# Vision tower, attention stage: the second layer norm's scaled rows computed by ScalarE instead of VectorE, and the output projection of a group issued one group later on TensorE

## The reference

```python
h = tok(x)                                   # (16, 37, 256)
h = h + attn(layernorm(h), w_qkv, w_o)       # 16 heads of 16, rotary, causal, softmax, @ w_o
h = h + ffn(layernorm(h), ...)               # gated MLP + product-key experts (top 8 of 4096)

def layernorm(x, eps=1e-5):
    return (x - mean(x)) / sqrt(var(x) + eps)
```

## Time and profile before

| | us |
|---|---|
| median of 3 plain runs | 273.3 (273.24 to 273.79) |
| profiled execution | 275.31 |
| its span, first to last instruction | 273.5 |
| busy PE / PEld / DVE / ACT / POOL | 247.0 / 203.7 / 180.7 / 57.0 / 54.7 |
| chain that ended last, shares | PE 58%, DVE 34%, ACT 3%, issue 3%, DMA 1% |
| mean granted TensorE clock | 0.975 of full |

### The profile page before, as it was taken

One profiled execution on the slowest core, in us unless ns is written; L12 is line 12 of the kernel. 1 busy time (PEld: TensorE's weight loads), 2 busy tenths in 40 slices (PEclk: granted clock), 3 DMA queues, 4 the chain that ended last, 5 costly groups with the idle time before them and its releaser, 6 DMA issues.

```text
span 273.5 us, 4832 instructions
## 1 busy us (share of the span) xinstructions
PE 247.0 (90%) x1956; PEld 203.7 (74%) x1956; DVE 180.7 (66%) x455; ACT 57.0 (21%) x104; POOL 54.7 (20%) x71
## 2 busy tenths in 40 slices
PE   3998985889768899899999999899979999999996
PEld 2575653668543488889898899888968888888773
DVE  0037199678885449999999999799968767511100
ACT  1101127343444242323132743100000000000000
POOL 5013146114422523225052620000000000000000
PEclk9999999999975799999999999999999999999999
DMA  7960000130002271061125430300000000000000
GB/s 253 386 233 0 2 0 0 55 104 29 25 20 74 63 218 54 7 205 60 40 54 178 127 105 1 91 0 2 0 19 2 0 19 2 0 19 2 19 0 12
DMA packets 14805, 16.99 MB, mean 62 GB/s; under 512 B 848, under 2 KB 12992, under 8 KB 14784
## 3 DMA queue, kind: packets, MB, share of 16 engines
q1 hardware_dynamic: 13776, 15.70, 17.9%
q10 hardware_dynamic: 1008, 1.00, 1.1%
HBM read 15.48 MB, written 1.21 MB: 61 GB/s over the span
## 4 chain that ended last, share of the span: by engine, by line
PE 58%; DVE 34%; issue 3%; ACT 3%; DMA 1%; DVEq 0%; POOL 0%; ACTq 0%
PE ps L1067 23%; PE ps L1030 9%; PE ps L820 7%; PE ps L1089 5%; DVE topi L696 3%; DVE big L795 3%; DVE top L693 3%; PE ps L971 3%; PE ps L1064 3%; DVE big L547 2%; PE ps L897 2%; DVE xn L515 2%; PE ps L938 2%; PE ps L847 2%; DVE red L589 1%
## 5 line engine op out<-in xcount | busy, mean ns | idle before, releaser
L1067 PE MATMUL ps<-ue,big 128*128 128x256 f32 (+1 forms) x320 | 72.3, 381 | 1.4 <-DVE big L795 1.4
L1067 PEld LDWEIGHTS ps<-ue,big 128*128 128x128 f32 (+1 forms) x320 | 57.2, 182 | 12.1 <-DVE big L795 1.8
L1030 PE MATMUL ps<-hn_hi,de_hi 128*128 128x296 f32 x128 | 40.7, 318 | 2.1 <-ACT big L482 1.1
L795 DVE TENSOR_TENSOR big<-ps,big 128x1024 f32<-128x1024 f32 (+1 forms) x19 | 22.7, 1197 | 26.9 <-PE ps L1089 26.2
L1030 PE MATMUL ps<-hn_lo,de_hi 128*128 128x296 f32 x128 | 38.4, 300 | 0.0
L1030 PE MATMUL ps<-hn_hi,de_lo 128*128 128x296 f32 x128 | 38.2, 299 | 0.0
L482 ACT ACTIVATE big<-ps 128x592 f32<-128x592 f32 x32 | 21.1, 665 | 44.5 <-PE ps L1030 44.4
L1030 PEld LDWEIGHTS ps<-hn_hi,de_hi 128*128 128x128 f32 x128 | 24.1, 188 | 4.7 <-DVE actT L742 1.9
L1030 PEld LDWEIGHTS ps<-hn_lo,de_hi 128*128 128x128 f32 x128 | 24.1, 188 | 1.2 <-issue 1.2
L1030 PEld LDWEIGHTS ps<-hn_hi,de_lo 128*128 128x128 f32 x128 | 24.1, 188 | 0.0
L820 PE MATMUL ps<-big 128*111 128x256 f32 (+1 forms) x72 | 19.3, 426 | 4.7 <-DMA big<-in_w_tok 4.7
(11 more groups left out here) (113 smaller groups left out, 337.9 us busy)
## 6 DMA issues: line engine op xcount, KB each, us to landing
de<-in_down_t SPq DMA_DIRECT2D x16, 256.0 KB, 2.8
ue<-in_up_e SPq DMA_DIRECT2D x4, 1024.0 KB, 5.9
big<-in_patches SPq DMA_DIRECT2D x6, 296.0 KB, 5.2
big<-in_w_tok ACTq DMA_DIRECT2D x6, 128.0 KB, 5.9
big<-in_w_qkv SPq DMA_DIRECT2D x1, 768.0 KB, 8.6
h_scratch<-big SPq DMA_DIRECT2D x5, 111.0 KB
late<-in_keys_bd SPq DMA_DIRECT2D x1, 512.0 KB, 9.7
downT<-in_wdown_t SPq DMA_DIRECT2D x1, 512.0 KB, 9.3
```

The source lines that it names most:

```text
L795: chain(nc.vector.tensor_tensor(dst, pv, dst, ALU.mult), g_ready)
L1030: last = mm(ps[:, 2 + 2 * (e % 2) + a, 0:HALF], half[:, (e // 2) % SPLITS, k, own], src[:, k, a * HALF:(a + 1) * HALF], start=(n == 0), st ...
L1067: last = mm(acc, sil[:, e, j * 128:j * 128 + Q * v], ue[:, e, :], start=False, stop=(e == EX - 1))
```

## The change

VectorE's `hidden_norm` goes. In its place POOL computes, after `rstd`, the value -mean times `rs` into a new tile `shift` (two one-column instructions, `rowshift`), and ACT computes `rs * h + shift` with one activation of the function Identity into `xn`. POOL runs `probabilities` one group further ahead of `rstd`. On PE `project` moves behind the scores of the next iteration, and `hidden_T` comes an iteration later; DVE's `hidden` and ACT's `hn_copy` follow. `hidden(g)` gets a wait for `hn_ready` before it overwrites `mv` and, through POOL, `rs` of two groups earlier.

```diff
 # POOL
+            def rowshift(gi):
+                r = GROUPS[gi][1] * S
+                nc.gpsimd.tensor_scalar(shift[0:r, gi % 2, 0:1], mv[0:r, gi % 2, 0:1], -1.0, None, ALU.mult
+                                        ).then_inc(shift_chain, 1)
+                pool.wait_ge(rstd_ready, NG + gi + 1)
+                pool.wait_ge(shift_chain, gi + 1)
+                nc.gpsimd.tensor_tensor(shift[0:r, gi % 2, 1:2], shift[0:r, gi % 2, 0:1], rs[0:r, gi % 2, :],
+                                        ALU.mult).then_inc(shift_ready, 1)
...
                     probabilities(0)
+                    probabilities(1)
                     for gi in range(NG):
-                        if gi + 1 < NG:
-                            probabilities(gi + 1)
+                        if gi + 2 < NG:
+                            probabilities(gi + 2)
                         rstd(NG + gi, gi)
+                        rowshift(gi)
 # ACT
+            def hidden_norm(gi):
+                r = GROUPS[gi][1] * S
+                act.wait_ge(shift_ready, gi + 1)
+                if gi >= 2:
+                    act.wait_ge(pe_hn, gi - 1)
+                nc.scalar.activation(xn[0:r, gi % 2, :], h[0:r, gi, :], ACT.Identity, bias=shift[0:r, gi % 2, 1:2],
+                                     scale=rs[0:r, gi % 2, :]).then_inc(hn_ready, 1)
...
-                if gi >= 2:
-                    hn_copy(gi - 2)
                 if gi + 2 < NG:
                     exponentials(gi + 2)
-
+                if gi >= 3:
+                    hn_copy(gi - 3)
+                if gi >= 2:
+                    hidden_norm(gi - 2)
+
+            hn_copy(NG - 3)
+            hidden_norm(NG - 2)
             hn_copy(NG - 2)
             act.wait_ge(s_zero, 2)
             for p in range(2):
                 act.wait_ge(pe_q, p + 1)
                 nc.scalar.copy(qT[:, p, 0:BANK], ps[:, 2 + p, :]).then_inc(qT_ready, 1)
+            hidden_norm(NG - 1)
             hn_copy(NG - 1)
 # DVE
                 chain(nc.vector.tensor_tensor(h[0:r, gi, :], ps[0:r, 7, 0:D], h[0:r, gi, :], ALU.add), h_ready)
+                if gi >= 2:
+                    dve.wait_ge(hn_ready, gi - 1)
                 moments(NG + gi, r, h[0:r, gi, :])
...
                 softmax_back(gi)
-                if gi >= 2:
-                    hidden_norm(gi - 2)
                 if gi + 1 < NG:
                     softmax_front(gi + 1)
                 else:
                     gated_rest(0)
                     gated_rest(1)
-                hidden(gi - 1)
-            hidden_norm(NG - 2)
+                if gi >= 2:
+                    hidden(gi - 2)
+            hidden(NG - 2)
             hidden(NG - 1)
             gated_rest(2)
-            hidden_norm(NG - 1)
             gated_rest(3)
 # PE
                 probs_T(gi)
-                if gi >= 2:
-                    hidden_T(gi - 2)
                 if gi + 2 < NG:
                     scores(gi + 2)
+                if gi >= 1:
+                    project(gi - 1)
+                if gi >= 3:
+                    hidden_T(gi - 3)
                 attend(gi)
-                project(gi)
+            hidden_T(NG - 3)
+            project(NG - 1)
             hidden_T(NG - 2)
```

More of the change, by code:

```diff
@@ L185, in vit_tower @@
         rs = sb("rs", [128, 2, 1])
+        shift = sb("shift", [128, 2, 2])
         veps, nhalf = sb("veps", [128, 2, 1]), sb("nhalf", [128, 1])
@@ L233, in vit_tower @@
         var_ready, rstd_ready = sem("var_ready"), sem("rstd_ready")
+        shift_chain, shift_ready = sem("shift_chain"), sem("shift_ready")
         dve_chain, pool_chain = sem("dve_chain"), sem("pool_chain")
@@ L610, in hidden @@
                 chain(nc.vector.tensor_tensor(h[0:r, gi, :], ps[0:r, 7, 0:D], h[0:r, gi, :], ALU.add), h_ready)
+                if gi >= 2:
+                    dve.wait_ge(hn_ready, gi - 1)
                 moments(NG + gi, r, h[0:r, gi, :])
-            def hidden_norm(gi):
-                r = GROUPS[gi][1] * S
-                if gi >= 2:
-                    dve.wait_ge(pe_hn, gi - 1)
-                scaled(NG + gi, r, h[0:r, gi, :], xn[0:r, gi % 2, :], hn_ready)
             def gated_rest(u):
```

## The result

The forecast was 1.8 us faster. The changed kernel is slower: 277.37 us as the median of six plain runs (274.71 to 278.07) against 273.31 (273.24 to 274.91), ratio 1.0114, 95% interval 1.0077 to 1.0151. Its profiled execution took 277.91 with a span of 276.1 (before 273.5).

The account below looks back on a forecast made before the run. VectorE, at 5.49 us a period, was taken to bound the loop. Queries at 84.4 + 6.1 + 1.7 + 1.12 = 93.3 against 95.05 gains 1.8, so 271.5 us from 273.3; range 267.4 to 273.2.

Parts of the forecast that it names:

- the 0.44: TensorE's idle time before project in each loop iteration, waiting for ScalarE's copy; claimed to go, making an iteration 4.61.
- the 1.43: VectorE's loop: time from the start of the second norm's scaling to the next maximum; its removal makes the period 4.06.
- The length of queries: First queries behind the loop, kept at its old 6.1 us; 3.7 at full clock, 7.4 all at the low level.
- The shift pair: GpSimd's two new one-column instructions per group, put at 0.44 to 1.14 us and taken as 0.80.
- The step that failed: Loop's tail: low clock from about 78 adds 0.95 on project(5) and some 0.4 behind it; queries at 84.0 before turns.
- 1.7 + 1.12: Tail: second queries starts 1.7 after the first ends, 0.8 later than before, and takes 1.12.
- the prediction's own sign of being wrong: Behind the second queries: an expert stage that does not move with them would show the forecast wrong.
- Taking turns: VectorE's gate subtractions of 75.0 to 76.9 meeting GpSimd's probabilities(5): 0.85 if they take turns, 0.4 taken.
- Full turns: Rival: gate subtractions and probabilities(5) take turns in full, all behind h_ready(3) 0.45 later than forecast, 271.9; chance 0.13.
- Slower: Rival: clock falls a group sooner, at the wait before transposes(4), 71.5 to 72.3; 1.5 lost, 274.8; chance 0.09.
- nothing comes of it: Rival: project's idle goes, but TensorE waits as long for GpSimd and later hidden rows eat the lead; 273.3; chance 0.06.
- The 0.2%: Some 0.55 us of the whole time, taken as what a measurement can tell from no change; chance within it 0.07.

Follow-up runs that it names:

- casts early: Changed kernel with group 5's scaling ahead of the copies of queries and ScalarE's four gate and up casts in groups 1 and 2; 273.77 us, ratio 0.9985.
- subtractions late: Changed kernel with group 5's scaling ahead of the copies of queries and VectorE's first two gate subtractions behind group 4's residual add; 272.24 us, ratio 0.9928.
- all waits filled: Changed kernel with extra unused matmuls in TensorE's waits over 0.6 us from group 5 on, also between the queries; 270.40 us, ratio 0.9860.
- mended kernel: Changed kernel, group 5's scaling and the casts earlier, two gate subtractions later, project(5) before group 3's hidden transposes; 271.97 us; A: attend(3) start to first queries.
- order alone: Changed kernel's lists, TensorE's new order included, with the scaling back on VectorE; 274.82 us, ratio 1.0019 to the kernel before.

## Why the prediction was wrong

*Right.* VectorE as the bound of the loop, the 0.44 and the 1.43 that go, no table loads, the schedule to attend of group 4 within 0.3, the fall of the clock near 78. The length of queries (6.18, forecast 6.1) was partly luck: it started near its old time, not at 84.4, and in kernels where it started earlier with the clock low it took 6.35 (casts early, 84.87) and 6.72 (subtractions late, 83.61). The shift pair cost less than taken (0.59, 65.85 to 66.44, forecast 0.80), the scaling more (0.58 to 0.62, forecast 0.42). That is some 1.5 times VectorE's 0.41, not three times. The Trainium skill (ScalarE: Activation LUTs, Rules for kernel authors) gives its factor of about three for bf16; these rows are fp32.

*The step that failed* is the sentence "With the clock low from about 78, project(5) takes 0.95 more, and transposes and hops behind it some 0.4". The low clock was charged to what stands on TensorE behind group 3's scaling, 1.0 in all, as if that scaling's rows were there at 80.45 (80.85 with the 0.4 for turns) whatever the clock. It ran from 82.16 to 82.78. At half the clock `project` of group 4 takes 2.02 (78.19), so attend of group 5 comes at 80.50, its copy on ScalarE at 81.05, and group 3's scaling stands behind that copy, a cast and two copies in ScalarE's list. The forecast had only GpSimd's shift (79.8) in front of it; after, that was ready at 80.40. Sizes: 86.62 against the forecast 84.4, 2.2 too early. The kernel with all waits filled, the same lists at the full clock, tells the parts apart. From attend of group 3 to group 3's scaling it takes 9.80 (70.39 to 80.19), the changed kernel 11.05 (71.11 to 82.16): the low clock costs 1.25 ahead of that scaling, which the forecast put at nothing. From there to queries the two take 3.48 and 4.46: 0.98 behind it, which is the 1.0 that was charged. The other 1.0 of the 2.2 stands at the full clock too: 0.2 by attend of group 3 (71.11, forecast 70.9), and 0.8 behind it, 13.28 against 12.5 (83.0 + 0.4 - 70.9). There, too, the scalings of groups 3 and 4 stand behind copies on ScalarE (they start at 80.19 and 81.86, their shifts are ready at 79.68 and 81.38) and take 0.6. The mended kernel shows that with the order changed the lead stays (A 11.96).

*The second term that was mis-sized* is the tail: 1.7 + 1.12. The gap was put at 0.8 more than before, and was 1.98 (92.80 to 94.78) against 0.91, 1.1 more, the scaling being 0.6. What was left out altogether is that the clock falls once more behind that gap, which it did not with the gap filled or halved: second queries 1.78 for 1.12, first expert block 4.23 for 3.52, together 1.4. The last matmuls of the tail were taken at the full rate without asking what the new gap does to the clock, although the working had just shown a gap doing it. Two sums: queries 2.2 late, 0.1 on its length, 0.3 on the gap and 0.66 on the second queries make 3.3, which is 96.56 against the forecast 93.3; 0.7 on the expert block and 0.4 further on make the span 4.4 longer than forecast (276.1 against 273.5 - 1.8 = 271.7). So the prediction's own sign of being wrong, an expert stage that does not move with the second queries, came true by 1.1.

*Taking turns*, put at 0.4 of 0.85, was nearly full: the first gate subtraction took 1.54 instead of 0.75, from 75.18, while GpSimd's probabilities ran:

```profile
74.99 1.17 POOL L356 TENSOR_TENSOR big<-big,red 37x592 f32<-37x592 f32 x1
...
80.21 0.19 POOL L349 TENSOR_TENSOR shift<-shift,rs 111x1 f32<-111x1 f32 x1
```

VectorE's residual add then came at 77.61 (forecast 76.9 plus 0.4). `project` of group 4 stands behind it, so some 0.3 of the miss lies here, and it lengthens the wait ahead of the fall. The Trainium skill (SBUF — State Buffer, SBUF: two separate sides) has this as a lock against a VectorE operation with two SBUF inputs. The row agrees (it began 0.19 behind the probabilities), and the second subtraction, behind them, took 0.70.

*The rivals.* 'Full turns' came true without its time. 'Slower' had its mechanism (TensorE at 1.2 GHz for longer) but the wrong place: it stood at the wait before group 4, and the second fall came more than 20 us later, behind the gap between the queries. That the 0.44 is worth nothing alone ('nothing comes of it') holds for the order alone, ratio 1.0019. The 0.2% taken as what a measurement can tell from no change was too fine: most intervals above reach 0.3 to 0.4% to either side.

*Open.* Some 0.4 us lie between the first top-8 matmuls and the end in every kernel with the scaling on ScalarE (175.4 to 175.6 against 175.0 to 175.1 with it on VectorE); it shows as a pause of 0.46 on VectorE in the fourth search (before 139.44 in the changed kernel), which no wait explains; another of 0.46 stands before 178.96. Neither is in the kernels with the scaling on VectorE, and the cause was not tried. Why the clock falls where it does is open as well.

## What to carry to other kernels

A step that an in-order engine takes over waits for everything in that engine's list: write down, for each moved item, what stands ahead of it and on which late producer that waits, and do it again with TensorE at its low clock, since a slower producer moves the items behind it on other engines too. Shortening a loop that feeds TensorE makes its tail emptier, and here that cost more than the loop gained; look for the last long waits before a dense stretch, move unrelated work out of the lists ahead of them, or fill them all, since one filled wait alone did not keep the clock full here. When two changes are made together, price each alone and the pair, with all else in the same place: here 1.8 gained, nothing, and together 3 lost, of which 2.5 came with the place of one small step.

## What the runs showed of the hardware that was not expected

The granted clock can fall under work that is already running: it fell at 95.05, 0.27 us into the second queries, after a stretch in which TensorE had done two short transposes in 2 us, and stayed low for 3.4 us of unbroken matmuls. With five extra matmuls in that stretch it did not fall. In the kernel before with one wait filled it fell at 73.25, 0.25 us into a `project` behind a wait of 0.43. The same code also differs in its mean clock from run to run: that kernel has 0.994 in plain runs near 270.7 us and 0.987 in those from 272.9 to 274.6, and one of the six plain runs of the changed kernel took 274.71 at 0.975, where the others have 0.968 or 0.969.

ScalarE's scaling of 256 columns with a bias and a scale per row took 0.58 to 0.62 from SBUF, where a scaled copy of as many columns out of PSUM took 0.46.
